# Value product of a windowed attention in 64x64 quadrants, with its transposes in the general PSUM banks

## What is computed

```
qkv = einsum('bsd,de->bse', h, Wqkv);  q, k, v = split(qkv, 3)       # 16 heads of 64
scores = einsum('bhsd,bhtd->bhst', q, k) * 64 ** -0.5
mask = (j >= i - 128 + 1) & (j <= i)
attn = softmax(where(mask, scores, -max))
out = einsum('bhst,bhtd->bhsd', attn, v);  out = out.reshape(b, s, 1024) @ Wout
x = x + ga * out
```

## Time and profile before

| | us |
|---|---|
| median of 3 runs | 1168.54 (1167.7 to 1168.84) |
| the profiled execution | 1170.37 |
| its span | 1168.7 |
| PE busy | 1096.9 (94%) |
| DVE busy | 766.3 (66%) |
| ACT busy | 662.3 (57%) |
| POOL busy | 507.5 (43%) |

### The profile page before, as it was taken

How to read it: one execution, slowest core, us unless ns; L and a number is a source line. 1 busy time by engine, 2 the same in 40 slices (tenths; PEclk the granted TensorE clock), 3 DMA queues, 4 the chain that set the end, 5 groups by cost and what they waited for, 6 DMA issues and landing times.

```text
span 1168.7 us, 25315 instructions
## 1 busy us (share of the span) xinstructions
PE 1096.9 (94%) x9508; PEld 718.8 (62%) x9508; DVE 766.3 (66%) x1693; ACT 662.3 (57%) x1876; POOL 507.5 (43%) x555
## 2 busy tenths in 40 slices
PE   6899999999999999999998894989999999999996
PEld 3355655655655655655656563665867768585865
DVE  6566587486586596586586675666666667576654
ACT  3377566476476476477475662637374654637361
POOL 3134254464364364365265455434343442525342
PEclk9999999999999999999999998999999999999998
DMA  9554001110110110000030004363254353524000
GB/s 331 108 169 138 2 19 20 37 29 20 43 23 16 42 20 24 32 20 24 27 92 32 19 8 138 88 147 72 97 100 140 62 143 120 118 100 85 22 20 9
DMA packets 119723, 80.60 MB, mean 69 GB/s; under 512 B 82856, under 2 KB 110642, under 8 KB 119348
## 3 DMA queue, kind: packets, MB, share of 16 engines
q1 hardware_dynamic: 108852, 57.46, 18.8%
q0 software_dynamic: 10752, 21.54, 6.4%
HBM read 39.49 MB, written 33.78 MB: 63 GB/s over the span
## 4 chain that ended last, share of the span: by engine, by line
PE 75%; issue 7%; DVE 7%; POOL 6%; ACT 4%; POOLq 0%; ACTq 0%; DVEq 0%
PE down L1510 18%; PE up L1496 17%; PE gen L556 10%; PE gen L647 6%; PE gen L570 6%; PE score L593 4%; PE pt L604 4%; PE pv L624 4%; PE pv L631 3%; ACT prob L851 2%; POOL probT_split L1315 2%; POOL probT_split L1317 1%; POOL h L361 1%; DVE prob L1026 1%; PE gen L655 1%
## 5 line engine op out<-in xcount | busy, mean ns | idle before, releaser
L1536 ACT ACTIVATE hid<-up,b1T 128x512 f16<-128x512 f32 (+2 forms) x192 | 122.4, 637 | 183.3 <-PE up L1496 180.4
L1496 PE MATMUL up<-xT,w 128*128 128x512 f16 (+2 forms) x1152 | 213.0, 346 | 13.0 <-issue 12.7
L1510 PE MATMUL down<-w,hid 128*128 128x256 f16 x1920 | 213.6, 274 | 3.2 <-DVE hid L1552 3.2
L1315 POOL TENSOR_SCALAR_AFFINE_SELECT probT_split<-probT 128x512 f32<-128x512 f32 x128 | 101.0, 789 | 254.3 <-ACT probT L859 250.1
L1510 PEld LDWEIGHTS down<-w,hid 128*128 128x128 f16 x1920 | 188.4, 98 | 27.7 <-DVE hid L1552 3.7
L556 PE MATMUL gen<-hT,big 128*128 128x512 f16 x768 | 185.5, 382 | 5.5 <-DVE hT L1275 2.9
L851 ACT ACTIVATE prob<-score,negmax 128x128 f32<-128x128 f32 x512 | 180.4, 373 | 7.6 <-DVE negmax L1018 7.5
L1496 PEld LDWEIGHTS up<-xT,w 128*128 128x128 f16 x1152 | 112.7, 98 | 107.7 <-issue 15.7
L1552 DVE TENSOR_TENSOR hid<-hid 128x512 f16<-128x512 f32 (+2 forms) x192 | 115.3, 607 | 91.6 <-ACT hid L1537 65.6
L1595 POOL DMA_INDIRECT out<-y,tail x80 | 82.2, 1028 | 207.4 <-DVE y L1580 193.9
L859 ACT ACTIVATE probT<-pt 128x512 f32<-128x512 f32 x128 | 76.8, 600 | 101.8 <-PE pt L604 101.0
(11 more groups left out here) (148 smaller groups left out, 1480.3 us busy)
## 6 DMA issues: line engine op xcount, KB each, us to landing
big<-in_L_ffn_W SPq DMA_DIRECT2D x14, 1024.0 KB
slot_inputs<-empty_row SPq DMA_DIRECT2D x80, 129.5 KB, 2.5
out<-x SPq DMA_DIRECT2D x7, 512.0 KB
x<-in_L_attn_x SPq DMA_DIRECT2D x1, 3072.0 KB, 22.0
q<-in_L_attn_Wqkv SPq DMA_DIRECT2D x2, 1024.0 KB, 8.1
kept<-out,tail POOLq DMA_INDIRECT x80
out<-y,tail POOLq DMA_INDIRECT x80
x<-in_L_attn_x SPq DMA_DIRECT2D x2, 512.0 KB, 9.0
```

The source lines that it names most:

```text
L1315: pool.affine_select(out=probT_split[:, h % 2, :, 1], in_=probT[:, h % 2], pattern=[[0, TILES], [1, P]], compare_op=ALU.is_ge, fill=zero, ...
L1496: mm = pe.matmul(bank, w1[:, par, kd, a, ft * P:(ft + 1) * P], part_rows(e, n, xT[:, par, b * KD + kd, :]), start=(i == 0), stop=(i == 5))
L1510: mm = pe.matmul(down[n][:, s, :], hid[:, ft, a, t * P:(t + 1) * P], w2[:, par, ft, b, :], start=(i == 0), stop=(i == 3 * FT - 1))
L1536: act.activation(part_rows(e, n, hid[:, ft, 0, :]), bank, ACT.Relu, scale=1 / W_SCALE, bias=bias).then_inc(hid_hi, 1)
```

## The change

1. `pt` is dropped; `pv` gets two banks. The transposes of chunks 0 to 6 become groups ("pt", h) of the two `gen` banks, listed in `chunk_groups` (and in `HEAD` for the first two units) at the place where PE issues them. They claim a bank, and `copy_probT` frees it. In the last chunk the units from 2 on use the second bank of `pv`, with pt_done and probT_ready as before. `copy_probT`, `exponentials` and `split_keys` wait on the new semaphores through `wait_turned`.
2. The value product of chunks 0 to 6 is issued by `quadrant_values` in two turns. Each turn has eight matmuls of 64 keys by 64 columns: per quadrant one of 128 query columns and one of 64. The half of each split tile that is zero is left out. Keys 0 to 63 and keys 64 to 127 write to different banks: in turn 0 the first half writes bank 0 and the second bank 1, in turn 1 the other way round, adding up. Turn 0 stands where the value product was, turn 1 (`other_values`) behind the transposes, after a wait for turn 0 (pv_half). pv_done is now set by turn 1; turn 0 of the second part of a pair waits for the pv_done of the first.
3. `attn_high` and `attn_low` read the pair from the two banks (`pv_pair`).
4. In ACT's queue `copy_probT` moves ahead of `ln_modulate` in step 5.
5. The small product of the conditioning (L486) uses `pv` instead of `pt`.

```diff
@@ -185,8 +185,7 @@
             score = [ps(f"score{i}", [P, TILES, 2 * P], F32) for i in range(2)]
-            pt = ps("pt", [P, TILES, P], F32)
-            pv = ps("pv", [P, CHUNK], F32)
+            pv = ps("pv", [P, 2, CHUNK], F32)
             gen = [ps(f"gen{i}", [P, 512], F32) for i in range(2)]
...
@@ -249,7 +248,7 @@
             HEAD_V = v_half(0) + v_half(1)
-            HEAD = [("ln0", 0), ("ln0", 1)] + HEAD_QK + ln_groups + HEAD_V
+            HEAD = [("ln0", 0), ("ln0", 1)] + HEAD_QK + ln_groups + HEAD_V[0:4] + [("pt", H)] + HEAD_V[4:6] + [("pt", H + 1)] + HEAD_V[6:]
 
...
@@ -288,7 +287,7 @@
                 for i in STEPS:
-                    names += [n for n in projections_at(c, i) if c == LAST]
+                    names += [("pt", i - 2)] if c != LAST else projections_at(c, i)
                     if c > 0:
...
@@ -316,6 +315,25 @@
 
+            def turned_in(c, h):
+
+                return (c - 1, ("pt", h + H)) if h < 2 else (c, ("pt", h))
+
+            def wait_turned(eng, u, copied):
+
+                c, h = u // H, u % H
+                if c == LAST and h >= 2:
+                    eng.wait_ge(probT_ready if copied else pt_done, h - 1)
+                else:
+                    bank, before = group(*turned_in(c, h))
+                    eng.wait_ge(gen_free[bank] if copied else gen_full[bank], before + 1)
+
+            def turned_bank(c, h):
+
+                if c == LAST and h >= 2:
+                    return pv[:, 1, :].rearrange("p (b q) -> p b q", q=P)
+                return gen[group(*turned_in(c, h))[0]][:].rearrange("p (b q) -> p b q", q=P)
+
             def starts_batch(c, b):
...
@@ -597,12 +620,38 @@
                     def transposes(c, h):
-                        u = H * c + h
-                        pe.wait_ge(norm_ready, u + 1)
-                        at_least(pe, probT_ready, u)
+                        if h >= H:
+                            c, h = c + 1, h - H
+                        pe.wait_ge(norm_ready, H * c + h + 1)
+                        if c < LAST or h < 2:
+                            full = claim(*turned_in(c, h))[1]
+                        else:
+                            full = pt_done
+                            at_least(pe, probT_ready, h - 2)
+                        dst = turned_bank(c, h)
                         for b in range(TILES):
-                            mm = pe.transpose(pt[:, b, :], prob[:, h % 2, b, :], identf[:])
-                        mm.then_inc(pt_done, 1)
+                            mm = pe.transpose(dst[:, b, :], prob[:, h % 2, b, :], identf[:])
+                        mm.then_inc(full, 1)
+
+                    def quadrant_values(c, u, turn):
+                        j, part = unit_of(c, u)
+                        for n in range(2):
+                            for half in range(2):
+                                i = (half + turn) % 2
+                                own = n == half
+                                lo, hi = (0, P) if n == 0 else (HALF * half, HALF * half + HALF)
+                                keys = slice(HALF * half, HALF * half + HALF)
+                                for hd in range(2):
+                                    r, h = DH * hd, 2 * j + hd
+                                    mm = pe.matmul(pv[r:r + DH, i, part * P + lo:part * P + hi],
+                                                   v[keys, 2 * part + i + own, h * DH:(h + 1) * DH],
+                                                   probT_split[keys, u % 2, 2 * hd + i, int(own), lo:hi],
+                                                   start=(turn == 0 and n == 0), stop=(turn == 1 and n == 1), skip_group_check=True)
+                        return mm
+
+                    def other_values(c, u):
+                        pe.wait_ge(pv_half, H * c + u + 1)
+                        quadrant_values(c, u, 1).then_inc(pv_done, 1)
 
...
@@ -618,17 +667,22 @@
                                 pe.wait_ge(gen_free[bank], before + 1)
+                        if c < LAST:
+                            if part == 1:
+                                pe.wait_ge(pv_done, n_unit)
+                            quadrant_values(c, u, 0).then_inc(pv_half, 1)
+                            return
                         par = u % 2
                         for hd in range(2):
                             r, h = DH * hd, 2 * j + hd
-                            mm = pe.matmul(pv[r:r + DH, 2 * part * P:(2 * part + 2) * P], v[:, 2 * part + 1, h * DH:(h + 1) * DH],
+                            mm = pe.matmul(pv[r:r + DH, 0, 2 * part * P:(2 * part + 2) * P], v[:, 2 * part + 1, h * DH:(h + 1) * DH],
                                            probT_split[:, par, 2 * hd:2 * hd + 2].rearrange("p a m q -> p (a m q)")[:, P:3 * P],
                                            start=True, stop=False, skip_group_check=True)
                         for i in range(2):
                             b = 2 * part + i
                             for hd in range(2):
                                 r, h = DH * hd, 2 * j + hd
-                                mm = pe.matmul(pv[r:r + DH, b * P:(b + 1) * P], v[:, b + i, h * DH:(h + 1) * DH],
+                                mm = pe.matmul(pv[r:r + DH, 0, b * P:(b + 1) * P], v[:, b + i, h * DH:(h + 1) * DH],
                                                probT_split[:, par, 2 * hd + i, i, :], start=False, stop=True,
...
@@ -726,6 +780,8 @@
                                 transposes(c, i - 2)
+                            if not last:
+                                other_values(c, i - 4)
                             if last:
...
@@ -846,7 +902,8 @@
                         act.wait_ge(maxed, u + 1)
-                        at_least(act, pt_done, u - 1)
+                        if u >= 2:
+                            wait_turned(act, u - 2, False)
                         for b in range(TILES):
...
@@ -854,15 +911,17 @@
                         u = H * c + h
-                        act.wait_ge(pt_done, u + 1)
+                        c, h = u // H, u % H
+                        wait_turned(act, u, False)
                         at_least(act, prev_ready, u - 1)
-                        act.activation(probT[:, h % 2], pt[:], ACT.Copy).then_inc(probT_ready, 1)
+                        copied = probT_ready if c == LAST and h >= 2 else gen_free[group(*turned_in(c, h))[0]]
+                        act.activation(probT[:, h % 2], turned_bank(c, h), ACT.Copy).then_inc(copied, 1)
 
                     def attn_high(c, j):
                         act.wait_ge(pv_done, H * c + 2 * j + 2)
                         if j == 0:
                             at_least(act, x2_ready, 2 * c)
-                        act.activation(attn[:, j, 0, :], pv[:], ACT.Copy).then_inc(attn_hi, 1)
+                        act.activation(attn_pair(j, 0), pv_pair, ACT.Copy).then_inc(attn_hi, 1)
 
...
@@ -930,10 +989,11 @@
                                 split_high(act, 0, 0, SPLIT_AT.index(i))
+                            if not last:
+                                copy_probT(c, i - 2)
                             if i == 5 and c + 2 < NC:
                                 ln_modulate(c, c + 2, "lnT")
                             if not last:
-                                copy_probT(c, i - 2)
                                 for name in projections_at(c, i):
...
@@ -1036,7 +1096,7 @@
                         dve.wait_ge(attn_hi, PAIRS * c + j + 1)
-                        dve.tensor_tensor(attn[:, j, 1, :], pv[:], attn[:, j, 0, :], ALU.subtract).then_inc(attn_lo, 1)
+                        dve.tensor_tensor(attn_pair(j, 1), pv_pair, attn_pair(j, 0), ALU.subtract).then_inc(attn_lo, 1)
 
...
@@ -1307,10 +1367,8 @@
                         u = H * c + h
-                        waits = [(probT_ready, u + 1)]
-                        if not isinstance(c, int) or u >= 2:
-                            waits.append((pv_done, u - 1))
-                        stand_ge(pool, *waits)
+                        wait_turned(pool, u, True)
+                        at_least(pool, pv_done, u - 1)
```

15 lines of the change are left out of this document (9 added, 6 removed).

## The result

The changed kernel takes 1174.95 us (median of 5 runs, 1174.68 to 1175.81) against 1168.54 (5 runs): ratio 1.0057, 95% interval 1.0043 to 1.0072, so it is 6.4 us slower. The forecast was 1174.7, range 1161 to 1184.

What follows compares the result with a forecast made beforehand. PE's queue was taken to bound the attention chunks. Terms -2.3 (free steps), +0.9 (stalled steps), +4.5 (step 15) and +3.1 (step 5) gave +6.2 us on the 1168.54 median: 1174.7 us, range 1161 to 1184.

Steps and rivals of the forecast that it cites:

- What bounds the kernel: Attention chunks: mostly PE's queue, 94% busy, with waits for split probabilities or attn_low, 19.1 us in the run.
- The free step: Step where PE never waits: 0.218 us saved, 0.155 for one more shape change; net -0.063, -2.3 us over 37.
- step 19: Value projection claims its bank at 3.52 us, copy done at about 3.57: the step's gain goes, 0.
- Rival A: PE's extra shape change is hidden, saving 0.22 us per unstalled step: 1162.4 us, 14%.
- ACT's order: Odd steps: attn_high waits for turn 1 and begins at 2.35 us, so the copy behind it ends at 3.51.
- step 15: Chunks 1 to 5: projection k5 claims the transposes' bank, starting at 3.57 us instead of 2.67; +4.5 us in all.
- Rival B: Bank claims don't bind, as the copy isn't held behind attn_high or comes in time: 1166.4 us, 12%.
- Step 5: Chunks 0 to 5: copy ahead of ln_modulate delays k0 to 4.31 us from 3.79; +0.52 each, +3.1 us in all.
- The stalled steps: Steps up to 14 whose value product waits on DVE and ACT chains: +0.045 us each, 19 in all, +0.9 us.
- rival C: Short matmul records are paced, a turn taking 0.43 us instead of 0.33: 1188.6 us, 10%.

Runs made afterwards that it cites:

- the experiment on the banks: Changed kernel, transposing DMAs replaced, with the old value product restored and transposes kept in the general banks: 1171.24 us, ratio 1.0029 to the kernel before.
- GpSimd light: GpSimd's four long operations per chunk cut to 8 columns, transposing DMAs replaced: kernel before 1159.54 us (ratio 0.9918), changed kernel 1177.51 us (1.0074).
- plain DMAs: Each transposing DMA replaced by an untransposed one of the same bytes: kernel before 1167.64 us (ratio 1.0003), changed kernel 1173.51 us (1.0053).
- the same quadrants, grouped: Changed kernel, transposing DMAs replaced, turns grouped by pairs around the scores, counts behind the projection: 1154.32 us, ratio 0.9884 to the kernel before.

## Why the prediction was right, and where it was not

**What bounds the kernel** held: in chunks 0 to 6 PE's queue, with three waits per chunk, and the loss came as waits for ACT, VectorE and GpSimd, not as PE's work.

**The free step** (-0.063) came out at -0.09. The four changes of shape cost 0.56 us together, 0.14 each, not 0.155: 3.62 less the streaming (0.66 + 0.33 + 0.44 + 0.33 + 1.30). Steps 6, 7, 10 and 11 and step 19 gain as much; I had given step 19 nothing, for a claim at 3.52 against a copy done at 3.57. The copy was done at 3.44, and no wait shows there. Rival A is out: the shape change is not hidden.

**ACT's order and step 15** held in mechanism and size (+0.84 of +0.90), shown from two sides: moving the counts and moving the copy each take it away. Some 0.5 of it comes with the shared bank alone, as the experiment on the banks shows, the rest with turn 1 behind the transposes. Rival B is out.

**Step 5** had the right mechanism and a term too large (+0.37 of +0.52). I had ACT's ln_modulate behind the copy's end plus a signal, at 3.57, and 0.73 us for its half. It starts before the copy's end, at 3.33, and k0 follows 0.84 later.

**The stalled steps** are the step of the prediction that failed: "+0.045 ... 19 in all" took it that the chains which end the waits keep their length while PE's work around them moves. For steps 6 to 9 that is nearly right (+0.07). For steps 10 to 12 it is +0.22 and for 13 and 14 +0.36, 0.5 us more per chunk than forecast. I had moved attn_high and the copy by 0.4 to 0.6 us in odd steps, and priced that only where PE claims the copy's bank. But what they hold back in ACT's queue also releases GpSimd, and so decides which VectorE operation runs beside which of GpSimd. GpSimd's queue from step 9 to step 12 of chunk 2, after and before:

```profile
259.73 2.06 POOL L393 TENSOR_TENSOR packed<-h,packed 128x1024 f16<-128x1024 f32 x1 [2.22 <-ACT packed L938]
...
262.92 1.09 POOL L1373 TENSOR_SCALAR_AFFINE_SELECT probT_split<-probT 128x512 f32<-128x512 f32 x1
...
267.10 1.08 POOL L1373 TENSOR_SCALAR_AFFINE_SELECT probT_split<-probT 128x512 f32<-128x512 f32 x1
```

```profile
257.26 2.07 POOL L370 TENSOR_TENSOR packed<-h,packed 128x1024 f16<-128x1024 f32 x1 [1.64 <-ACT packed L879]
...
260.59 0.63 POOL L1315 TENSOR_SCALAR_AFFINE_SELECT probT_split<-probT 128x512 f32<-128x512 f32 x1
...
264.98 1.08 POOL L1315 TENSOR_SCALAR_AFFINE_SELECT probT_split<-probT 128x512 f32<-128x512 f32 x1
```

GpSimd's packed, which waits for ACT, begins 4.33 us into step 9 instead of 3.81, because attn_high, ahead of it in ACT's queue, starts 0.50 us later. From there GpSimd's queue runs without a pause, and one half of a split in it takes 1.09 us instead of 0.63: it stands beside the normalise, which VectorE had begun 0.20 us earlier (0.07 later in the kernel before). So its operation on hT begins 2.02 us into step 11 instead of 1.78, and the first half of the split in step 12 ends at 1.57 instead of 1.23 (scores at 266.61 and 264.83). PE waits for it: turn 0 starts at 1.88, the value product before at 1.55. With GpSimd light that stretch loses nothing. In step 13 it is the split and L1144. What I had asked of every bank, who is late next, I hadn't asked of GpSimd.

The Trainium skill has the rule (SBUF — State Buffer, Who interferes with whom): a VectorE instruction with two inputs in SBUF and a GpSimd instruction that reads SBUF exclude each other for a whole instruction, while tensor_reduce doesn't contend. The trace agrees: L1144, L1157 and L1086 end just behind GpSimd's operation, while the tensor_reduce L1078 of step 10 keeps its 0.66 us beside a split, in step 13 a reciprocal and four MAX8 keep their 0.18 and 0.37, and so does attn_low in step 12 (0.68 us), which reads one input from PSUM. With the two places found, the sum would have been 5 x 0.5 = 2.5 us larger.

**What cancelled it.** The sum came out at +6.2 and the measurement at +6.4 partly by luck. Of the terms in chunks 1 to 5, the stalled stretches cost 2.5 us more than forecast, and the other rows of the table 2.0 less (steps 5, 15 and 19 and the free ones); chunk 4 adds 0.2, and chunk 0 gained 0.4 more than forecast (its steps from 6 to 19 are nearly all free). The 1.47 of chunk 6 are mostly not the change. Of them, 1.39 is one step, 18 (4.88 to 3.49 us), and 1.25 of that is a fall of the clock in the profiled execution of the kernel before. A stretch of it (the granted clock is the number ahead of the last two) and its value product:

```profile
627.40:630.00 2.60, 2.60 (x16) 1.75 (x13) 2.12 (x4) 0.77 (x5) 2.29 (x3) 0.50 0.13 47
...
627.21 1.02 PE L624 MATMUL pv<-probT_split,v 128*64 128x256 f32 x4 [1.15 <-DVE attn L1039]
```

The same value product in the kernel before with plain DMAs, where the step takes 3.63 us:

```profile
627.66 0.65 PE L624 MATMUL pv<-probT_split,v 128*64 128x256 f32 x4 [1.15 <-DVE attn L1039]
```

The granted clock is 0.50 in the one and full in the other. The kernel before with GpSimd light has plain DMAs and shows the same fall (4.78 us), so it isn't a matter of the transposing DMAs. PE had waited 0.37 and 1.15 us in that step, with plain DMAs just as long, and there the clock stayed full; so what sets off the fall isn't shown. Without this fall chunk 6 gains 0.22, as forecast, and chunks 0 to 6 lose 7.45 - 0.56 - 0.22 = 6.67 us, for 6.4 in the timed runs. With plain DMAs they lose 6.2, for 5.9.

**The Trainium skill's overhead of 60 cycles per matmul** (TensorEngine Tiling (Array Packing), Instruction Overhead), weighed under rival C, does not show here as an addition to each matmul: sixteen more records of a turn add 0.34 us where nothing waits, and halving the columns of half of them saves the 0.21 us that streaming alone gives.

## What to carry to other kernels

When a stage moves by a few tenths of a microsecond, follow each thing that it releases, not only the next claim of the same bank: here some 2.5 of the 6.4 us came from GpSimd's queue, late behind ACT's and sliding over two-input operations of VectorE. Count changes of array shape per step and try the order that groups equal shapes across neighbouring steps before giving up a better tiling: the same quadrants, grouped, went from +5.9 to -13.8 us (3.0 of the difference by the counts' place). Sharing a buffer turns the place of its reader in another engine's queue into a term of the critical path.

## What the runs showed of the hardware

- A two-input VectorE operation on SBUF tensors waits out GpSimd's instruction and ends a fixed time behind it: 0.04 us for 128x32, 0.55 for 128x512 (the normalise of step 11 beside hT, before and after). Where VectorE begins first, GpSimd waits: its split takes 1.09 us instead of 0.63. A wait that was to avoid one such meeting made another, longer one (1.16 us instead of 0.29).
- The granted clock can fall to half, 1.2 GHz, while PE has work. In seven of the fourteen profiles it did so in chunks 1 to 6, for 3.4 us at a time (once 6.8), at a cost of 1.2 to 1.7 us where the step can be compared. Waits of PE stood ahead of every fall, but the same waits stand in other chunks and kernels without one. So a single profiled execution can be off by such a piece: read the clock of the stretch before a difference of 1 to 2 us is explained.
- A wait of PE for its own last result costs 0.33 us where nothing lies between.
- Less work on GpSimd did not make the changed kernel faster: PE pauses for 1.2 to 1.8 us in step 17, with no releaser in the profile. It is not explained.
